# Mamba scan, mixture of experts and FFN on one core: experts on tokens sorted by expert, in blocks of 128

## The reference

```
delta = softplus(x @ Wd + bd);  B = x @ WB + bB;  C = x @ WC + bC;  A = -exp(A_log)      # 16 states
for each token t of a batch, for each of the 128 channels and 16 states:
    h = clip(exp(min(delta*A, 2)) * h + clip(delta*B, -2, 2) * x, -100, 100)
    y = sum_s(h * C) + x * D_param
routing = softmax(y @ Wr + br)            # 4 experts
top1_w, top1_i = max(routing), argmax(routing)
all_out[e] = silu(y @ up_w[e] + up_b[e]) @ down_w[e] + down_b[e]     # 128 -> 512 -> 128
attn = norm(y + all_out[top1_i] * top1_w) * ln_w + ln_b
x1 = norm(x + attn)
out = norm(x1 + (silu(x1 @ wg) * (x1 @ wu)) @ wd)       # 128 -> 384 -> 128, integer weights / 127
```

## Time and profile before

| | us |
|---|---|
| median of 3 runs (1068.84 to 1071.22) | 1071.18 |
| the profiled execution | 1072.12 |
| its span | 1069.6 |
| mean granted TensorE clock | 0.879 of full |
| VectorE busy | 877.5 |
| TensorE busy | 839.0 |
| ScalarE, GpSimd busy | 610.2, 561.4 |

### The profile page before, as it was taken

The page is one execution under the profiler, slowest core; times in us unless marked ns, Lnnn a source line. Parts: engine busy times, 40 slices in busy tenths (PEclk is TensorE's granted clock), DMA queues, the critical chain, the costliest instruction groups (busy, mean ns, idle before and its releaser), DMA issues.

```text
span 1069.6 us, 12973 instructions
## 1 busy us (share of the span) xinstructions
PE 839.0 (78%) x4059; PEld 523.2 (49%) x4120; DVE 877.5 (82%) x1173; ACT 610.2 (57%) x838; POOL 561.4 (52%) x412
## 2 busy tenths in 40 slices
PE   2354599768888789858897789869897789989973
PEld 1010256446555455646555455546554555657552
DVE  4999988699898998989899898889899999962332
ACT  5362177446856378546866278456775367625432
POOL 1255356545657365555666466564576466644232
PEclk8565699879998899989998899979998799989996
DMA  4100100010000100010000100001000000000000
GB/s 134 40 1 1 59 1 1 1 49 12 10 1 11 50 21 1 1 55 16 10 0 10 50 10 10 0 11 49 20 0 10 30 11 11 17 4 21 1 10 20
DMA packets 23039, 20.60 MB, mean 19 GB/s; under 512 B 2227, under 2 KB 19891, under 8 KB 22966
## 3 DMA queue, kind: packets, MB, share of 16 engines
q1 hardware_dynamic: 22966, 19.84, 5.9%
HBM read 15.64 MB, written 4.19 MB: 19 GB/s over the span
## 4 chain that ended last, share of the span: by engine, by line
PE 37%; DVE 36%; issue 15%; ACT 8%; POOL 2%; DVEq 1%; SPq 0%; DMA 0%; ACTq 0%; POOLq 0%
PE psU L442 15%; DVE state L854 12%; DVE psB L667 8%; PE psD L456 6%; DVE prod L863 3%; PE psU L475 3%; PE psB L387 3%; ACT decay L569 2%; DVE bst L796 2%; DVE weighed L774 2%; PE psU L402 2%; PE psU L476 2%; PE psT L456 2%; PE psC L387 1%; DVE top_w L761 1%
## 5 line engine op out<-in xcount | busy, mean ns | idle before, releaser
L945 POOL TENSOR_TENSOR yacc<-prod,yacc 128x1024 f32<-128x1024 f32 x112 | 271.1, 2421 | 173.0 <-DVE prod L863 172.6
L854 DVE TENSOR_TENSOR_SCAN state<-decay,psB 128x1024 f32<-128x1024 f32 x128 | 292.8, 2287 | 13.2
L587 ACT ACTIVATE hid<-psU,upb_sb 128x512 f32<-128x512 f32 x256 | 176.1, 688 | 223.0 <-PE psU L442 222.8
L442 PE MATMUL psU<-y,up_sb 128*128 128x512 f32 x512 | 265.5, 656 | 0.6 <-ACT hid L587 0.6
L387 PE MATMUL psB<-bc_parts,sel 128*128 128x512 bf16 x233 | 83.7, 438 | 130.7 <-DVE state L854 102.2
L863 DVE TENSOR_TENSOR prod<-state,psC 128x1024 f32<-128x1024 f32 x128 | 156.0, 1219 | 22.3 <-PE psC L387 15.8
L667 DVE TENSOR_TENSOR psB<-dx,psB 128x1024 f32<-128x1024 f32 x128 | 156.6, 1224 | 16.5 <-PE psB L387 15.0
L456 PEld LDWEIGHTS psD<-down_sb,hid 128*128 128x128 f32 x1280 | 161.9, 205 | 7.3 <-issue 2.7
L442 PEld LDWEIGHTS psU<-y,up_sb 128*128 128x128 f32 x512 | 95.8, 206 | 139.5 <-ACT hid L587 92.8
L456 PE MATMUL psD<-down_sb,hid 128*128 128x128 f32 x1280 | 161.3, 288 | 0.2
L569 ACT ACTIVATE decay<-next_delta,a_sb 128x1024 f32<-128x1024 f32 x128 | 136.5, 1138 | 1.5 <-DVE state L854 1.4
(11 more groups left out here) (118 smaller groups left out, 1130.0 us busy)
## 6 DMA issues: line engine op xcount, KB each, us to landing
xT_sb<-in_xT SPq DMA_DIRECT2D x8, 512.0 KB, 3.6
x_again<-in_xT SPq DMA_DIRECT2D x8, 512.0 KB, 4.5
xt<-in_x SPq DMA_DIRECT2D x16, 256.0 KB, 3.5
out<-x SPq DMA_DIRECT2D x16, 256.0 KB, 2.3
up_sb<-in_up_w SPq DMA_DIRECT2D x1, 1024.0 KB, 7.5
hid<-in_wg SPq DMA_DIRECT2D x1, 192.0 KB, 2.4
hid<-in_wu SPq DMA_DIRECT2D x1, 192.0 KB, 2.5
hid<-in_wdn SPq DMA_DIRECT2D x1, 192.0 KB, 2.9
```

Of the source, the lines that this page charges most:

```text
L442: pe.matmul(bank[banks[f]][:, :], up_sb[:, e, f * 128:(f + 1) * 128], half(y, c), start=True, stop=True).then_inc(filled[banks[f]], 1)
L587: nc.scalar.activation(hid[:, k % 2, f, :], bank[u][:, :], ACT.Silu, bias=upb_sb[:, (k % E) * NF + f:(k % E) * NF + f + 1]).then_inc(drain ...
L854: v.tensor_tensor_scan(state[:, :], decay[:, s % NDECAY, :], psB[:, :], 0.0, ALU.mult, ALU.add).then_inc(state_ready, 1)
L945: g.tensor_tensor((y if s == S - 1 else yacc)[:, :], prod[:, s % NPROD, :], (xD if s == 0 else yacc)[:, :], ALU.add).then_inc(added, 1)
```

## The change

After the router, the tokens of a batch are sorted by expert. Each expert gets whole blocks of 128 slots; 8 blocks of tokens and at most 3 more for the remainders make NBLK = 11. Ranks come from TensorE: the one-hot choice (`chosen`, bf16) is multiplied by a strictly triangular matrix and by ones (`rank`). `slots` on VectorE works out each token's slot and each block's expert. Eight indirect DMAs from GpSimd (`scatter`) write the 8 groups of 128 token rows to a DRAM tensor `rows_in`, SP reads it back sorted (`y_sorted`, in GROUPS of 4, 4 and 3 blocks), TensorE turns it (`sort_turn`), ScalarE copies it. Then each of the 11 blocks goes through `up`, `silu`, `down` of one expert, whose weights and biases SP loads from `w_pack` (128 x 1156 floats, 592 KB) into one of three buffers, by an expert number read into a register. `result` adds the bias on VectorE, SP stores the blocks to `rows_out`, eight indirect DMAs (`gather`) bring each token its row back in the next iteration, and `combine` on VectorE multiplies by `top_w` and adds `y`. `weigh`, `mix`, `up_sb`, `down_sb` and the bias product go. All of both halves' norms 0 and 1 move to iteration C, and so do x_turn 0 and FFN half 0, to later steps. `out` is stored from ScalarE's queue. All iterations are written out; the register loop goes.

The diff, cut to its core:

```diff
-            for i in range(-1, FIRST_FULL):
-                body(Iteration(i))
-            with eng.Fori(FIRST_FULL, LAST_FULL + 1) as i:
-                body(Iteration(i))
-            for i in range(LAST_FULL + 1, NB + 2):
+            for i in range(-1, NB + 2):
                 body(Iteration(i))
...
 PE_STEPS = [
+    (0, 'B', 'y_turn'), (5, 'B', 'rank'), (10, 'P', 'z'), (11, 'P', 'bc'), (13, 'P', 'b_turn'),
+    (14, 'B', 'sort_turn', 0), (14, 'B', 'sort_turn', 1), (15, 'B', 'sort_turn', 2), (15, 'B', 'up', 0),
+    (15, 'C', 'x_turn', 0), (16, 'B', 'up', 1), (16, 'B', 'down', 0), (17, 'B', 'up', 2), (17, 'B', 'down', 1),
+    (17, 'C', 'ff_up', 0), (18, 'B', 'up', 3), (18, 'B', 'down', 2), (19, 'B', 'up', 4), (19, 'B', 'down', 3),
+    (20, 'C', 'ff_down', 0), (20, 'B', 'up', 5), (20, 'B', 'down', 4), (21, 'B', 'up', 6), (21, 'B', 'down', 5),
+    (22, 'C', 'x_turn', 1), (22, 'B', 'up', 7), (22, 'B', 'down', 6), (23, 'C', 'ff_up', 1),
+    (24, 'B', 'up', 8), (24, 'B', 'down', 7), (24, 'P', 'b_spread', 0), (25, 'P', 'b_spread', 1),
+    (25, 'B', 'up', 9), (25, 'B', 'down', 8), (26, 'C', 'ff_down', 1), (26, 'B', 'up', 10), (26, 'B', 'down', 9),
+    (28, 'B', 'down', 10), (30, 'P', 'flag'),
 ACT_STEPS = [
+    (14, 'C', 'norm', 1, 0), (14, 'B', 'sort_copy', 0), (15, 'B', 'sort_copy', 1),
...
+    (19, 'B', 'silu', 4), (19, 'A', 'decay', 12, 16), (20, 'B', 'silu', 5), (20, 'C', 'norm', 1, 1),
+    (21, 'B', 'silu', 6), (22, 'C', 'x_high', 1), (22, 'B', 'silu', 7), (22, 'C', 'norm', 0, 2),
 DVE_STEPS = [
+    (2, 'B', 'router_shift'), (4, 'B', 'router_pick'), (6, 'B', 'slots'),
+    (10, 'C', 'combine', 0), (10, 'C', 'stats', 0, 0), (13, 'C', 'combine', 1), (13, 'C', 'stats', 1, 0),
+    (14, 'P', 'b_max'), (14, 'C', 'stats', 0, 1), (16, 'C', 'x_low', 0), (17, 'P', 'bc_low'),
+    (17, 'B', 'result', 0), (18, 'C', 'ff_mul', 0), (18, 'B', 'result', 1), (19, 'B', 'result', 2),
+    (19, 'C', 'stats', 1, 1), (20, 'B', 'result', 3), (20, 'P', 'delta'),
+    (21, 'C', 'ff_sum', 0), (21, 'B', 'result', 4), (22, 'B', 'result', 5), (22, 'C', 'x_low', 1), (23, 'B', 'result', 6),
+    (24, 'C', 'ff_mul', 1), (24, 'B', 'result', 7), (24, 'P', 'bound', 0), (26, 'P', 'bound', 1),
+    (26, 'B', 'result', 8), (27, 'C', 'ff_sum', 1), (27, 'B', 'result', 9), (28, 'P', 'majorant'),
+    (29, 'B', 'result', 10), (30, 'P', 'flag'),
 POOL_STEPS = [
+    (2, 'C', 'gather', 0), (2, 'C', 'gather', 1), (3, 'C', 'gather', 2), (3, 'C', 'gather', 3),
+    (4, 'C', 'gather', 4), (4, 'C', 'gather', 5), (5, 'C', 'gather', 6), (5, 'C', 'gather', 7),
+    (7, 'B', 'scatter', 0), (7, 'B', 'scatter', 1), (8, 'B', 'scatter', 2), (8, 'B', 'scatter', 3),
+    (9, 'B', 'scatter', 4), (9, 'B', 'scatter', 5), (10, 'B', 'scatter', 6), (10, 'B', 'scatter', 7),
...
+            def load_weights(b, k):
+                q = NBLK * b + k
+                if k == 0:
+                    sp_.wait_ge(blocks_ready, b + 1)
+                wait(sp_, result_ready, q - NW + 1)
+                e = sp_.value_load(block_expert[0:1, b % 2, k:k + 1], min_val=0, max_val=E - 1)
+                sp_.dma_start(weights[:, q % NW, :], w_pack[bass.ds(e, 1), :, :].rearrange("o p w -> p (o w)")
+                              ).then_inc(weights_in[q % NW], 16)
...
+                if it.runs["B"]:
+                    b = it.b["B"]
+                    for k in range(NW):
+                        load_weights(b, k)
+                    sp_.wait_ge(scattered, 16 * 2 * NJ * (b + 1))
+                    wait(sp_, turned, len(GROUPS) * b)
+                    for g, (k0, k1) in enumerate(GROUPS):
+                        sp_.dma_start(y_sorted[:, k0:k1, :], rows_in.rearrange("(k p) d -> p k d", p=ROWS)[:, k0:k1, :]
+                                      ).then_inc(sorted_in[g], 16)
+                    for k in range(NW, NBLK):
+                        load_weights(b, k)
+                        if k == NW + 3:
+                            store(b, 0)
+                    store(b, 1)
+                    store(b, 2)
...
+                if name == "rank":
+                    pe.matmul(bank["T"][:, 0:n], lower[:, :], one_hot, start=True, stop=False, skip_group_check=True)
+                    for r in range(1, 2 * NJ):
+                        pe.matmul(bank["T"][:, r * E:n], onesb[:, :], one_hot[:, 0:n - r * E], start=False,
+                                  stop=False, skip_group_check=True)
+                    for j in range(2 * NJ):
+                        mm = pe.matmul(bank["T"][:, n:n + E], onesb[:, :], chosen[:, j, :], start=False,
+                                       stop=(j == 2 * NJ - 1), skip_group_check=True)
...
                 if name == "up":
+                    pe.wait_ge(weights_in[q % NW], 16 * (q // NW + 1))
+                    pe.wait_ge(turned, len(GROUPS) * b + g + 1)
                     for f in range(NF):
+                        mm = pe.matmul(bank[u][:, f * ROWS:(f + 1) * ROWS], weights[:, q % NW, f * 128:(f + 1) * 128],
+                                       yT_sorted[:, k, :], start=True, stop=True)
                 if name == "down":
+                    for f in range(NF):
+                        mm = pe.matmul(bank[d][:, 0:D], hid[:, k % 2, f, :],
+                                       weights[:, q % NW, W_DOWN + f * D:W_DOWN + (f + 1) * D],
+                                       start=(f == 0), stop=(f == NF - 1))
...
+                if name == "result":
+                    dve.wait_ge(filled[d], it.fills(d, "B", ("down", k)))
+                    v.tensor_tensor(result[:, k, :], bank[d][:, 0:D], weights[:, q % NW, W_DOWNB:W_DOWNB + D], ALU.add
                                     ).then_inc(drained[d], 1)
+                    dve.wait_ge(drained[d], it.fills(d, "B", ("down", k)))
+                    dve.sem_inc(result_ready, 1)
+                if name == "combine":
+                    dve.wait_ge(gathered, 16 * 2 * NJ * (b + 1))
+                    for j in range(NJ):
+                        ins = v.scalar_tensor_tensor(out=moe[:, c, j, :], in0=chosen_out[:, n, :],
+                                                     scalar=top_w[:, b % 2, n:n + 1], in1=ytok[:, b % 2, n, 0:D],
+                                                     op0=ALU.mult, op1=ALU.add)
...
+                if name == "scatter":
+                    if n == 0:
+                        pool.wait_ge(slots_ready, b + 1)
+                    g.indirect_dma_start(rows_in, bass.IndirectOffsetOnAxis(slot[:, b % 2, n:n + 1].bitcast(U32), 0),
+                                         ytok[:, b % 2, n, 0:D], None).then_inc(scattered, 16)
+                if name == "gather":
+                    if n == 0:
+                        pool.wait_ge(stored, 16 * len(GROUPS) * (b + 1))
+                    g.indirect_dma_start(chosen_out[:, n, :], None, rows_out,
+                                         bass.IndirectOffsetOnAxis(slot[:, b % 2, n:n + 1].bitcast(U32), 0)
+                                         ).then_inc(gathered, 16)
```

320 lines of the change are left out of this document (205 added, 115 removed), and 37 rows, old and new, of tables (ACT_STEPS, DVE_STEPS, PE_STEPS, POOL_STEPS).

## The result

The change makes the kernel slower: 1204.95 us (median of 4 runs, 1201.09 to 1207.83) against 1070.01, a ratio of 1.1265 with a 95% interval of 1.1241 to 1.1289. The forecast was 1117 us with a range of 1040 to 1190. The sign was right; the size was not, and the time lies outside the range. The profiled execution took 1206.61, its span is 1204.8, 135.2 more than before.

What follows compares the result with a forecast made beforehand. VectorE was taken to bound iterations with a scan, TensorE only the tail. A full iteration was 120.3 + 6.2 work - 5.3 waits + 5.5 stalls = 126.7; seven of these plus 230 gave 1117 us, range 1040 to 1190.

Steps and rivals of the forecast that it cites:

- What bounds the kernel; TensorE's gift: VectorE sets the time in iterations with a scan; TensorE sheds some 35 us, of which 5.3 of waits reach VectorE.
- VectorE's work, +6.2: VectorE per iteration: 6.6 us gone; added `result` 4.4, `combine` 1.8, `slots` 1.6 and contention with GpSimd 5.
- Stalls, "I take 5.5": New VectorE waits per full iteration: late decays about 2.5 and a handoff about 3; ends 0 and 15 us.
- The handoff x_turn, x_high, x_low ... about 3: Part of the stalls: x_turn, x_high, x_low, `ff_up 1` stand in the same in-order row, about 3 us.
- The decays: ScalarE's decays 12 to 15 and table loads between `silu 4` and `silu 5`, 7.1 us, make `result 5` about 2.5 late.
- Loads, "just covered": Expert weights per block, 5.0 us from `result` to landed weights, just covered by FFN work moved beside them on VectorE.
- Scatter and gather, "cost 0 here": Sixteen indirect DMAs on GpSimd at 1.3 us each: the chain to `sort_turn 0` just fits, cost 0 per iteration.
- The tail, 140: After the last scan product: 82 us to the last expert product's end, 16 for store and gathers, 42 after; before 121.9.
- A: Rival: GpSimd's DMAs are dear; at 2.2 us each a full iteration is about 137, total 1185; chance 0.20.
- 7T + 230: Total time in us, T being the length of a full iteration, forecast at 126.7; breaks even at 120.3.
- B (faster): Rival: TensorE's relief reaches VectorE, nothing new stops it; iteration 115, total 1035 us; chance 0.21.
- C, the clock: Rival: with less work TensorE's granted clock falls; iteration 5 us longer, tail 8, total 1160; chance 0.13.

Runs made afterwards that it cites:

- before_unrolled: The kernel before with its register loop written out and nothing else changed: 1067.41 us, ratio 0.9989.
- norm_first: The changed kernel with the chain of norms of half 0 begun earlier on VectorE, GpSimd, ScalarE and TensorE: 1192.02 us, ratio 1.1125 to the kernel before.
- delta_late: The changed kernel with only `delta` moved from VectorE's step 20 to step 23: 1190.95 us, ratio 1.1115 to the kernel before.
- eight_orders: The changed kernel with plain unsorted copies, three weight loads, eight blocks, norms earlier, `delta` later, epsilon addition moved to GpSimd: 1065.28 us, ratio 0.9961 to the kernel before.
- norm_delta_plain_static: norm_delta with plain DMAs from SP in place of the indirect ones (rows unsorted) and only the first three weight loads: 1124.55 us.
- before_indirect: The kernel before, loop written out, plus sixteen indirect DMAs per batch at the changed kernel's GpSimd steps, their result unread: 1141.31 us, ratio 1.0660.
- norm_delta: The changed kernel with both new orders, norm_first's and delta_late's: 1187.05 us, ratio 1.1099 to the kernel before.
- warm: The changed kernel with unneeded 512-column TensorE products before each `psC` spread, four per state, later two: 1207.68 us, ratio 1.1286 to the kernel before.

## Why the prediction was wrong, step by step

The prediction's span was 1114.6; measured are 1204.8, 90.2 more: five full iterations +65.2, batch 7's +10.5, tail +13.2, the second iteration +1.8, the start -0.5. A full iteration was to be 126.7 and the one in the stage rows above is 140.1: 1.4 of the 13.4 come from the base (120.3 was one short iteration of before; the mean of before_unrolled is 121.0), -3.5 from VectorE's work and 15.5 from idle time.

**What bounds the kernel; TensorE's gift.** Right. TensorE shed 25 us per iteration and not 35: the up and down products of eleven blocks take 28.0, not 20, and the spreads of B and C 24.7 where they took 17.9 before, at a granted clock of 0.73 against 0.92. Of the two waits of the earlier trace rows that it could give back all but 0.9 is gone.

**VectorE's work, +6.2.** Too high: +2.7. `result` is 0.28 and the gap behind it, in which it waits for its own end, mostly 0.24 to 0.34; the `chosen` that should stay contended took 0.19, and `passed` and `place` in `slots` 0.20 and 0.18. Contention was there in other places (one of the two `combine` groups of an iteration takes 3.0; `dx` 3.4 where it was 1.2 before, in exchange for the earlier trace rows's long copies).

**Stalls, "I take 5.5".** This is the step that failed. Idle time was to be 13.4 - 5.3 + 5.5 = 13.6 and is 29.1; even my upper end of 15 would have given only 23.1. Three parts of it:

- "The handoff x_turn, x_high, x_low ... about 3": 9.5. As written, with `ff_up 1` at its end, it is the hand-off of half 1, whose wait is 1.4; that of half 0, 8.1, stands in no term. The change had put the whole chain of half 0, from `combine` on, into one iteration, and its first link waits behind the scatters on GpSimd (2.3 of the 9.5 go with them). norm_first removes the wait: VectorE's idle time falls by 7.7, but its busy time rises by 4.6, most of it in one `ve` of 4.9 us.
- The decays: I had them hold `down` 5 and `result` 5 by 2.5. They hold `delta` by 4.3, because it overwrites what they read; delta_late moves it and gains 2.7 per iteration. I had named what stands behind the decays and not who writes their input. Without the loads the wait is 2.2; why it halves was not followed up.
- Eleven small rounds of up, `silu`, down and `result` instead of eight large ones: 2.0 us per block, of which VectorE's work and gap are 0.6. My sum had the 0.4 of work and took the wait as covered by the FFN.

**Loads, "just covered".** Nearly right in an iteration (2.5), and 7 in the tail, where three waits for weights of 3.4, 3.4 and 4.3 stand in the chain below. From the end of a `result` to the `up` that waited for its buffer are 4.2 to 5.2 us there (5.0 foretold).

**Scatter and gather, "cost 0 here".** The duration was right, 0.97 and a gap of 0.30 where the earlier trace rows had led me to 1.3:

```profile
L1035 POOL DMA_INDIRECT rows_in<-ytok,slot x64 | 62.7, 979 | 19.9 <-issue 17.6
...
L1042 POOL DMA_INDIRECT chosen_out<-rows_out,slot x64 | 61.6, 962 | 19.1 <-issue 13.6
```

The zero was not. I checked the one consumer that the rows are for, and `sort_turn` indeed was not held by them in any full iteration. I did not ask who stands behind sixteen DMAs in GpSimd's row. By themselves, in the kernel before, they cost 10.8 per iteration at these steps and 0.2 at others; in the changed kernel, with other tasks behind them, 3.3 (why less was not tested).

**The tail, 140.** 153.2. From the end of the last product of the scan to the end of the last expert product 87.2 (82 foretold), store and gathers 14.1 (16), the rest 51.9 (42), since now norms and FFN of both halves stand behind the gathers. From the chain that ended last in the kernel after:

```profile
1102.74 3.41 DMA weights<-in_w_pack
...
1115.90 3.39 DMA weights<-in_w_pack
...
1130.78 4.32 DMA weights<-in_w_pack
...
1139.16 2.09 DMA rows_out<-result
1141.53 0.80 POOL chosen_out L1042
...
1150.39 2.49 DMA chosen_out<-rows_out,slot
```

**Rivals.** A comes nearest, for a wrong reason: it needs a DMA of 2.2 us, and it is 1.27 with its gap. Its sum is wrong as well: by 7T + 230, a T of 137 and a tail 12 longer give 1201, not 1185. The range should then have reached above 1190, and that 1204.95 lies close to 1201 is luck. B (faster) was wrong in that nothing new would stop the relief: it did reach VectorE, and new waits took its place. C, the clock: it did fall, from 0.94 to 0.73 in a full iteration, but what it costs was not separated. In one full iteration `ff_down` 1 took 4.18 us and VectorE waited 2.9 for it, while `ff_down` 0 took 2.84; on the other side stands eight_orders, with 122.2 us per iteration at the same clock. How the 131 us of norm_delta_plain_static split between blocks, clock and hand-offs is open beyond the 2.0 to 2.9 per block (2.9 with the moved addition).

## What to carry to other kernels

Price a task on an in-order engine by who stands behind it there, not by the engine's idle sum: the same sixteen DMAs of a batch cost 74 us in all in one order and 5 in another. Where a change moves a chain into one iteration, add up all its links from its first input, and for every late engine list both who reads what it makes and who overwrites what it reads. When a wait is taken away, look at the busy time too: instructions that stand still beside GpSimd grow, and no list of waits shows it. Less arithmetic in more, smaller steps is no gain on an engine that is not the bound; count the steps that the bounding engine must stand in line for.

## What the runs showed of the hardware

- An indirect DMA of 128 rows of 512 bytes holds GpSimd for 0.96 to 0.98 us on average, and the next one starts 0.30 us later. In before_indirect they land a median of 2.2 (to DRAM) and 2.5 us (from it) after issue; GpSimd does not wait for that. (The Trainium skill, DMA: Bandwidth & Descriptors, section Anatomy of one DMA, gives about 2.0 us fixed per DMA from this queue, most of it completion latency; by that rule these landings and the tail's 2.49 agree, and none of it is GpSimd's time.)
- In norm_delta one VectorE instruction on 128x4 elements took from 0.17 to 5.10 us; the five long ones (4.9 to 5.1, one in each full iteration) overlap a scatter and the two GpSimd instructions behind it.
- 14 us more of TensorE work per iteration (77 to 91, warm) raised the mean granted clock by only 0.04.
